# Weight chunks of two of three loaders cast on VectorE, and the third loader issued from ScalarE

## The chip, the cores and the metric

The kernel runs on the 8 cores of one Trainium2 chip (trn2), the same program on each with its own part of the batch, and no exchange between them. The metric is device time in microseconds of the slowest core. Engines: PE is TensorE (matmuls and transposes), ACT is ScalarE, DVE is VectorE, SP is SyncE, which here only issues transfers, POOL is GpSimd, used at the start alone.

## The reference

An input x of 32 sequences of 2048 rows and 1024 columns (f32) goes through four layers, each added to its input:

```python
x = x + attn_a(layernorm(x))   # q, k = xWq+bq, xWk+bk; softmax(q k^T / 32) + eye - mean; times layernorm(x)
x = x + ffn(layernorm(x))      # sigmoid(xr Wr) * (relu(xk Wk)^2 Wv); xr, xk mix a row with the row before
x = x + attn_b(layernorm(x))   # 8 heads of 128, four segments of 512 rows, a memory M, z carried on
x = x + ffn(layernorm(x))      # the same weights as the first ffn
```

Each weight is 1024 x 1024 in f32: wqa and wka of the first attention, wr, wkf and wvf of the FFN, wqb, wkb and wvb of attention b.

## The kernel before

A core computes four sequences, one after the other. A sequence lies whole in SBUF (`x_tm`, 16 tiles of 128 rows, f32), and goes through attention a, FFN (f1), attention b (ab) and FFN (f2) there. Products are in bf16.

**Order.** The program is written out by hand by a planner (`Plan`): each call appends an instruction to the list of its engine, with the semaphore values that it waits for. An engine runs its list strictly in this order, so an instruction that waits holds up all that stands behind it. `dv`, `ac`, `mm_group`, `tr_group` append to DVE, ACT and PE; `sy_dma` and `sc_dma` append a transfer to SP's and to ACT's list. `sy_dma` waits for all earlier transfers of SP (semaphores sXD, sST), and `sc_dma` for all earlier ones of ACT (sGD), so each of the two lists has one transfer in flight.

**Weights.** SBUF has room for three weights in bf16 (`warena`, slots 0 to 2), and they are loaded anew for each layer of each sequence. A `LoadW` loads one in 8 steps, from chunk c = 7 down to 0: a step transfers 128 x 1024 in f32 (512 KB) to a staging place and casts it to bf16 into `warena[:, slot, c, :]`. The staging place is the free front part of the slot itself for c >= 2, and the shared buffer `wst0` for c = 1 and 0, where a transfer waits for the cast that used it before (`buf_war["wst"]`). A step's transfer waits for the cast of the step before. q = 0 has the transfer issued by SP, q = 1 by ACT. The cast was ACT's `activation(Identity)` in both cases (L305). `arm` puts a loader on a list with a gate, all that PE, ACT and DVE have been given up to then; `wstep()` makes one step of each armed loader at this place of the program, and `fin()` the steps that are left.

**Where the steps stand.**

- At the start of the kernel `LKA.fin()` loads wka in 8 steps, ahead of the normalised tiles.
- In the scores loop of attention a, 16 tiles c in four groups of four (order 2, 3, 0, 1): each tile has `wstep()`, `emit_scores` (four products for one bank each, banks 0 and 1 in turn, each freed by an exp on ACT, L537), and `emit_tail` of the tile before (DVE's L549, L553 and L556 make `nzcol`, which PE transposes; PE transposes the exps, DVE copies them (L580), PE multiplies, DVE adds to `x_tm` (L596), then `stats_tile`: DVE's sum L348 and ACT's square L351). Groups 0 and 1 of the loop carry the 8 steps of wkf, group 3 four steps of wr, groups without a loader none.
- After the loop wvf is armed and has one step behind the last tail; `emit_ffn` finishes wr and wvf with `fin()` right after `ln_stats` and before the normalised tiles (`ln_apply`: even tiles on ACT L415, odd ones on DVE L419), for which PE's transposes wait.
- The FFN runs per group of 512 rows: `s12` (normalise, transpose, mix), `s3` (products with wr and wkf), `s4` (8 products with wvf, each evacuated by DVE's L763 out of banks 0 and 1 in turn; then per tile transposes back, two DVE adds L784, and a hook). In the last `s4` there is a `wstep()` ahead of each of the 8 products: wqb and wkb after f1, the next sequence's wqa and wka after f2. The hook after f1 is `stats_tile`; after f2 it stores the tile, loads the next sequence's tile in its place, both on SP, and takes `stats_tile` of that.
- wvb is armed after the last `s4` of f1, and `fin()` in `emit_attn_b` makes all its 8 steps, after `ln_stats` and before two memsets and the normalised tiles.
- Attention b handles a segment head by head: `passA_g(h + 1)` and `passB_g(h)` are interleaved, with a `wstep()` ahead of each h. In the last segment wr, wkf and wvf for f2 are armed together, so each of the 8 steps handles three chunks. `passB_g` begins with two ACT operations (L987, L991) and DVE's L994.

Of the kernel before, what the change touches and what calls it, by code (L numbers as in the profile page):

```python
# [9 lines left out]
AF = mybir.ActivationFunctionType  # L10
# [79 lines left out]
def build_nc(n_sub=4, dbg=False, ffn_level=None):  # L90
# [11 lines left out]
    wvfT_d = nc.dram_tensor("wvfT", [D, D], F32, kind="ExternalInput").ap()  # L102
    wqb_d = nc.dram_tensor("wqb", [D, D], F32, kind="ExternalInput").ap()
    wkb_d = nc.dram_tensor("wkb", [D, D], F32, kind="ExternalInput").ap()
    wvb_d = nc.dram_tensor("wvb", [D, D], F32, kind="ExternalInput").ap()
# [19 lines left out]
    warena = sb("warena", [P, 3, NC, D], BF16)  # L125
# [68 lines left out]
    def dv(fn, waits=(), tag="", inc=True):  # L194
        return p_.add("vector", fn, waits=waits, inc=("sDV" if inc else None), tag=tag)

    def ac(fn, waits=(), tag="", inc=True):
        return p_.add("scalar", fn, waits=waits, inc=("sAC" if inc else None), tag=tag)
# [30 lines left out]
    def gp_dma(out, in_, waits=(), tag=""):  # L229
        waits = list(waits) + [p_.cur("sGD")]  # L230
        def f(e, out=out, in_=in_):
# [10 lines left out]
       waits=[m1], tag="identb")  # L242
# [4 lines left out]
       waits=[mt], tag="tril")  # L247
# [4 lines left out]
       waits=[m2], tag="identf")  # L252
# [13 lines left out]
                              func=AF.Sigmoid), waits=[sm_ready], tag="gate")  # L266
# [6 lines left out]
       tag="negbq")  # L273
    dv(lambda e: e.tensor_scalar(out=dsm[:, 7, :], in0=smalls[:, 5, :],
                                 scalar1=-1.0, scalar2=None, op0=ALU.mult),
       tag="negbk")
# [5 lines left out]
    class LoadW:  # L282
# [7 lines left out]
        def step(self):  # L290
            if self.c < 0:
                return
            c = self.c
            self.c -= 1
            dma = sy_dma if self.q == 0 else sc_dma
            wf = warena.ap()[:, self.slot, :, :].rearrange(
                "p c e -> p (c e)").bitcast(F32)
            stage = wf[:, 0:1024] if c >= 2 else wst0.ap()
            w = list(self.gate) + ([self.last] if self.last else [])
            if c < 2:  # L300
                w = w + buf_war.get("wst", [])
            ld = dma(stage, self.dram_ap[128 * c:128 * (c + 1), :], waits=w,
                     tag=f"{self.tag}c{c}")
            self.last = ac(lambda e, slot=self.slot, c=c, stage=stage:
                           e.activation(out=warena[:, slot, c, :], in_=stage,  # L305
                                        func=AF.Identity),
                           waits=[ld], tag=f"{self.tag}x{c}")
            if c < 2:
                buf_war["wst"] = [self.last]
            if self.c < 0:  # L310
                self.mile = self.last
# [25 lines left out]
    for b in range(BL):  # L337
        if n_sub >= 4 and b > 0:
            x_ready = []
        else:  # L340
            xw = [p_.cur("sST")]
            x_mile = sy_dma(x_tm[:], x_d[b].rearrange("(t p) d -> p t d", p=P),
                            waits=xw, tag=f"ldx{b}")
# [93 lines left out]
        def fm_transpose_group(g, buf, src_tiles, xn_m, tag, guard_from=None):  # L437
            miles = []
            tm = None
            for half in range(4):  # L440
# [17 lines left out]
                else:  # L458
                    def f(e, bnk=bnk, buf=buf, dc0=dc0):
# [9 lines left out]
                              tag=f"b{b}ln1_")  # L469
# [8 lines left out]
        if n_sub >= 2:  # L478
            f1_ldrs = (LoadW(wrT_d, 0, 0, f"b{b}f1_ldwr"),
                       LoadW(wkfT_d, 1, 1, f"b{b}f1_ldwk"),  # L480
                       LoadW(wvfT_d, 2, 0, f"b{b}f1_ldwv"))
        else:
            f1_ldrs = None
        w_ka = LKA.fin()
# [7 lines left out]
        for g in range(NG):  # L492
            fm_m, _ = fm_transpose_group(g, g % 2, [4 * g + t for t in range(4)],
                                         xn_m[4 * g + 2:4 * g + 4],
                                         tag=f"b{b}a1g{g}")
            for ec in range(NC):
# [4 lines left out]
                def f(e, bnk=bnk, ec=ec, g=g):  # L501
# [4 lines left out]
                                    tag=f"b{b}Kev{g}_{ec}"))  # L506
# [4 lines left out]
        for dh in range(2):  # L511
# [3 lines left out]
                          tag=f"b{b}cs{dh}")  # L515
# [92 lines left out]
        for gi, g in enumerate([2, 3, 0, 1]):  # L608
            if gi >= 2:
# [3 lines left out]
                                             tag=f"b{b}a2g{g}")  # L613
# [3 lines left out]
            for ec in range(NC):  # L617
# [4 lines left out]
                def f(e, bnk=bnk, ec=ec):  # L622
# [4 lines left out]
                                 tag=f"b{b}Qev{g}_{ec}"))  # L627
            if gi == 3 and f1_ldrs:
                arm(f1_ldrs[0], slot_free_gate())
            for c4 in range(4):  # L630
                c = 4 * g + c4
# [503 lines left out]
        if n_sub >= 3:  # L1135
            ab_ldrs = (LoadW(wqb_d, 0, 0, f"b{b}ab_ldwq"),
                       LoadW(wkb_d, 1, 1, f"b{b}ab_ldwk"),
                       LoadW(wvb_d, 2, 0, f"b{b}ab_ldwv"))
        f2_ldrs = None
        if n_sub >= 4:  # L1140
            f2_ldrs = (LoadW(wrT_d, 0, 0, f"b{b}f2_ldwr"),
                       LoadW(wkfT_d, 1, 1, f"b{b}f2_ldwk"),
                       LoadW(wvfT_d, 2, 0, f"b{b}f2_ldwv"))
        nseq = None
        if n_sub >= 4 and b + 1 < BL:
            carry_qa = LoadW(wqaT_d, 0, 0, f"b{b + 1}ldwqa")
# [28 lines left out]
        if n_sub < 4:  # L1175
            st_w = p_.barrier_waits("sDV", "sAC", "sPE")
            sy_dma(out_d[b].rearrange("(t p) d -> p t d", p=P), x_tm[:],
                   waits=st_w, store=True, tag=f"st{b}")
# [3 lines left out]
           waits=[("sST", 16 * NSTORE), p_.cur("sGD"), p_.cur("sXD")],  # L1182
           tag="final")
# [66 lines left out]
if __name__ == "__main__":  # L1250
    nc = build_nc()
    print("built OK")
```

How the kernel before makes its waits and increments, by code:

```python
    def hard_barrier(tag=""):  # L210
        arr = {}
        for e in ("tensor", "vector", "scalar", "gpsimd"):
            s = p_.eng_sem[e]
            def mk(s=s):
                return lambda en: en.sem_inc(sems[s], 1)
            arr[e] = p_.add(e, mk(), inc=s, tag=f"{tag}barA", attach=False)
        dmaw = [p_.cur("sGD"), p_.cur("sXD"), p_.cur("sST")]
        allw = list(arr.values()) + dmaw
        for e in ("tensor", "vector", "scalar", "gpsimd", "sync"):
            p_.add(e, (lambda en: en.wait_ge(sems["sGP"], 1)), waits=allw,
                   tag=f"{tag}barW")
# [969 lines left out]
            def body(eng):  # L1191
                for (fn, w, incs, tag) in p_.ops[eng_name]:
                    for (s, v) in w:
                        eng.wait_ge(sems[s], v)
                    inst = fn(eng)
                    for (s, v, a) in incs:
                        if a:
                            inst = inst.then_inc(sems[s], v)
```

## Time and profile before

| | us |
|---|---|
| two timed runs | 9316.83 and 9549.73 |
| their median | 9433.28 |
| the profiled execution | 9315.16 |
| its span on the slowest core (core 2) | 9313.5 |
| spans of cores 0 to 3 | 9287.9 to 9313.5 |
| spans of cores 4 to 7 | 9217.3 to 9237.7 |
| PE busy | 5086.6 (55%) |
| DVE busy | 3046.4 (33%) |
| ACT busy | 2712.0 (29%) |
| mean granted TensorE clock, core 2 and core 6 | 0.725 and 0.735 |

The profile is of one execution. "Busy" leaves out issuing and waiting; idle time of an engine is listed with what ended it, the releaser. Lines such as L305 are lines of the kernel; ACTq and SPq are the issues of transfers by ACT and SP. The granted clock is a share of full speed, 1.0 for 2.4 GHz and 0.5 for 1.2 GHz.

### The profile page before, as it was taken

The numbers are of one execution on the slowest core, as the hardware profiler recorded it, in microseconds if no ns is written. First come the engines' busy times: TensorE is split into PE (matmuls) and PEld (weight loads), VectorE is DVE, ScalarE is ACT, GpSimd is POOL, SyncE is SP. The second block draws the span as 40 slices with busy tenths as digits, with TensorE's granted clock in tenths as the row PEclk, the third lists the DMA queues.
The fourth block names the chain that finished last, engine by engine and source line by source line (L and its number), as shares of the span: only waits on it lengthen the run. The fifth ranks groups of instructions, "written<-read, shape, count | busy, mean of one in ns | idle before, by whom it ended". The sixth has DMA issues, their size and how long they took to land.

```text
span 9313.5 us, 79467 instructions; the slowest of 8 cores (9217.3 to 9313.5 us)
## 1 busy us (share of the span) xinstructions
PE 5086.6 (55%) x26253; PEld 2480.5 (27%) x26688; DVE 3046.4 (33%) x6569; ACT 2712.0 (29%) x4642; POOL 8.6 (0%) x14
## 2 busy tenths in 40 slices
PE   3856444435586644443558563444355866444437
PEld 1323222212232322221223232222122323222213
DVE  2124244343112424434312242443431124244343
ACT  3222333321322233332132223333213222333321
POOL 0000000000000000000000000000000000000000
PEclk9988766667798866666779786555677977755558
DMA  2010100111101010011110101001011010100000
GB/s 73 19 37 1 55 1 1 32 35 43 57 17 37 1 55 1 1 39 34 36 59 14 37 7 48 1 1 39 34 36 57 16 37 1 55 1 1 25 30 37
DMA packets 69421, 256.82 MB, mean 28 GB/s; under 512 B 7584, under 2 KB 7584, under 8 KB 69024
## 3 DMA queue, kind: packets, MB, share of 16 engines
q1 hardware_dynamic: 50592, 184.60, 6.0%
q10 hardware_dynamic: 18432, 67.12, 2.3%
q8 instruction: 225, 3.69, 0.2%
q14 instruction: 172, 1.41, 0.1%
HBM read 218.14 MB, written 33.55 MB: 27 GB/s over the span
## 4 chain that ended last, share of the span: by engine, by line
PE 45%; DVE 18%; ACT 13%; DMA 12%; issue 10%; DVEq 1%; ACTq 0%; SPq 0%
PE pb L170 37%; PE pb L183 6%; DVE a L699 4%; PE pb L943 2%; ACT warena L305 2%; DMA x_tm<-x 2%; DMA warena<-wkfT 2%; DVE a L692 2%; ACT xn_fm L460 1%; ACT xn_tm L991 1%; DMA out<-x_tm 1%; ACT ptbuf L928 1%; ACT xn_tm L987 1%; DVE ebuf L911 1%; DMA warena<-wqb 1%
## 5 line engine op out<-in xcount | busy, mean ns | idle before, releaser
L170 PE MATMUL pb<-a,warena 128*128 128x512 bf16 x6013 | 1431.1, 396 | 372.1 <-DVE a L699 157.6
L170 PE MATMUL pb<-xn_fm,warena 128*128 128x512 bf16 x5000 | 1209.5, 405 | 92.7 <-ACT xn_fm L460 59.2
L170 PEld LDWEIGHTS pb<-a,warena 128*128 128x128 bf16 x6144 | 613.5, 101 | 1167.5 <-issue 580.3
L183 PE MATMUL pb<-identb,xn_tm 128*128 128x128 bf16 x2304 | 243.0, 281 | 1098.9 <-ACT xn_tm L415 780.2
L183 PE MATMUL pb<-identb,ebuf 128*128 128x128 bf16 x2304 | 285.8, 261 | 1009.7 <-DVE ebuf L911 1009.7
L351 ACT ACTIVATE junkb<-x_tm 128x1024 bf16<-128x1024 f32 x256 | 270.4, 1056 | 1935.1 <-DMA x_tm<-x 688.1
L170 PE MATMUL pb<-ebuf,warena 128*128 128x512 bf16 x1992 | 529.5, 430 | 420.6 <-DVE a L763 387.8
L170 PEld LDWEIGHTS pb<-xn_fm,warena 128*128 128x128 bf16 x5120 | 523.3, 103 | 765.8 <-issue 344.6
L183 PEld LDWEIGHTS pb<-identb,xn_tm 128*128 128x128 bf16 x2304 | 200.0, 127 | 1150.3 <-issue 1148.0
L170 PE MATMUL pb<-xn_tm,ptbuf 128*128 128x512 bf16 x1984 | 458.0, 384 | 81.1 <-DVE ptbuf L580 76.1
L905 ACT ACTIVATE ebuf<-pb 128x128 bf16<-128x128 f32 (+3 forms) x512 | 221.5, 433 | 924.2 <-PE pb L170 698.3
L183 PEld LDWEIGHTS pb<-identb,ebuf 128*128 128x128 bf16 x2304 | 165.0, 109 | 1159.2 <-issue 1154.6
L348 DVE TENSOR_REDUCE stats<-x_tm 128x1 f32<-128x1024 f32 x256 | 306.3, 1217 | 439.7 <-DMA x_tm<-x 424.1
L170 PE MATMUL pb<-a 128*128 128x128 bf16 (+4 forms) x2496 | 430.9, 271 | 7.8 <-DVE xn_tm L1006 7.8
L305 ACT ACTIVATE warena<-warena 128x1024 bf16<-128x1024 f32 x264 | 275.7, 1054 | 488.2 <-DMA warena<-wkfT 109.5
L170 PEld LDWEIGHTS pb<-ebuf,warena 128*128 128x128 bf16 x2048 | 219.2, 109 | 725.6 <-issue 566.0
L862 ACT ACTIVATE a<-pb,smalls_s 128x512 bf16<-128x512 f32 x384 | 263.8, 687 | 483.9 <-PE pb L170 483.9
L699 DVE SCALAR_TENSOR_TENSOR a<-xn_fm,smalls_s,a 128x512 bf16<-128x512 bf16 x512 | 384.6, 751 | 54.9 <-DVE a L692 1.8
L943 PE MATMUL pb<-xn_tm,ptbuf 128*128 128x128 bf16 x1280 | 215.9, 291 | 335.6 <-ACT ptbuf L928 183.3
L743 DVE TENSOR_TENSOR ebuf<-ebuf 128x4096 bf16<-128x4096 bf16 x32 | 73.3, 2292 | 914.0 <-ACT ebuf L733 914.0
L183 PE MATMUL pb<-identf,a 128*128 128x128 f32 x1024 | 173.9, 314 | 348.7 <-DVE x_tm L784 318.5
L456 DVE COPY xn_fm<-pb 128x1024 bf16<-128x1024 bf16 x144 | 99.4, 691 | 676.8 <-PE pb L183 676.8
(101 smaller groups left out, 5286.1 us busy)
## 6 DMA issues: line engine op xcount, KB each, us to landing
out<-x_tm SPq DMA_DIRECT2D x64, 512.0 KB, 2.6
warena<-wkfT ACTq DMA_DIRECT2D x48, 512.0 KB, 3.5
warena<-wrT SPq DMA_DIRECT2D x48, 512.0 KB, 3.6
warena<-wvfT SPq DMA_DIRECT2D x48, 512.0 KB, 3.4
x_tm<-x SPq DMA_DIRECT2D x48, 512.0 KB, 3.5
warena<-wqaT SPq DMA_DIRECT2D x24, 512.0 KB, 4.3
warena<-wkaT ACTq DMA_DIRECT2D x24, 512.0 KB, 3.6
warena<-wqb SPq DMA_DIRECT2D x24, 512.0 KB, 4.7
```

The lines of the kernel that those rows point to most:

```text
L170: return e.matmul(out, lhsT, rhs, start=st, stop=sp)
L183: return e.transpose(out, in_, ident)
L305: e.activation(out=warena[:, slot, c, :], in_=stage, func=AF.Identity),
L348: s1m = dv(lambda e, i=i: e.tensor_reduce(stats[:, i, 0:1], x_tm[:, i, :], axis=AX.X, op=ALU.add), waits=w, tag=f"{tag}S1_{i}")
L351: s2m = ac(lambda e, i=i: e.activation(out=junkb.ap(), in_=x_tm[:, i, :], func=AF.Square, accum_out=stats[:, i, 1:2]), waits=w + buf_war.g ...
L456: return e.tensor_copy(xn_fm[:, buf, dc0:dc0 + 2, 4:516], pbb[bnk][:, 0:1024])
L460: return e.copy(xn_fm[:, buf, dc0:dc0 + 2, 4:516], pbb[bnk][:, 0:1024])
L692: e.tensor_scalar(out=xrxk[:, u, dc, :], in0=xn_fm[:, buf, dc, 3:515], scalar1=dsm[:, omcol, dc:dc + 1], scalar2=None, op0=ALU.mult),
L699: e.scalar_tensor_tensor(out=xrxk[:, u, dc, :], in0=xn_fm[:, buf, dc, 4:516], scalar=smalls[:, mucol, dc:dc + 1], in1=xrxk[:, u, dc, :], o ...
L862: e.activation(out=sqkv[:, u, ec, :], in_=pb[bnk].ap(), func=AF.Identity, bias=smalls[:, bcol, ec:ec + 1]),
L905: e.activation(out=Eslot[:, 0:ncols], in_=pb[sb_].ap()[:, 0:ncols], func=AF.Exp, scale=1.0 / np.sqrt(DK)),
L943: return e.matmul(pb[4].ap()[:, 128 * lc:128 * lc + 128], ptbuf[:, j, :], xn_tm[:, 4 + j, 128 * h:128 * h + 128], start=st, stop=sp)
```

## The change

- A loader with q = 1 has its cast made by DVE (`tensor_copy`) instead of ACT; one with q = 0 keeps ACT's `activation`.
- wvf (f1 and f2) and wvb change from q = 0 to q = 1: their transfers are issued by ACT, and their casts are DVE's.

The steps stand where they stood, and the order of all else is the same.

```diff
--- before.py
+++ after.py
@@ -301,10 +301,15 @@
                 w = w + buf_war.get("wst", [])
             ld = dma(stage, self.dram_ap[128 * c:128 * (c + 1), :], waits=w,
                      tag=f"{self.tag}c{c}")
-            self.last = ac(lambda e, slot=self.slot, c=c, stage=stage:
-                           e.activation(out=warena[:, slot, c, :], in_=stage,
-                                        func=AF.Identity),
-                           waits=[ld], tag=f"{self.tag}x{c}")
+            if self.q == 0:
+                self.last = ac(lambda e, slot=self.slot, c=c, stage=stage:
+                               e.activation(out=warena[:, slot, c, :],
+                                            in_=stage, func=AF.Identity),
+                               waits=[ld], tag=f"{self.tag}x{c}")
+            else:
+                self.last = dv(lambda e, slot=self.slot, c=c, stage=stage:
+                               e.tensor_copy(warena[:, slot, c, :], stage),
+                               waits=[ld], tag=f"{self.tag}x{c}")
             if c < 2:
                 buf_war["wst"] = [self.last]
             if self.c < 0:
@@ -478,7 +483,7 @@
         if n_sub >= 2:
             f1_ldrs = (LoadW(wrT_d, 0, 0, f"b{b}f1_ldwr"),
                        LoadW(wkfT_d, 1, 1, f"b{b}f1_ldwk"),
-                       LoadW(wvfT_d, 2, 0, f"b{b}f1_ldwv"))
+                       LoadW(wvfT_d, 2, 1, f"b{b}f1_ldwv"))
         else:
             f1_ldrs = None
         w_ka = LKA.fin()
@@ -1135,12 +1140,12 @@
         if n_sub >= 3:
             ab_ldrs = (LoadW(wqb_d, 0, 0, f"b{b}ab_ldwq"),
                        LoadW(wkb_d, 1, 1, f"b{b}ab_ldwk"),
-                       LoadW(wvb_d, 2, 0, f"b{b}ab_ldwv"))
+                       LoadW(wvb_d, 2, 1, f"b{b}ab_ldwv"))
         f2_ldrs = None
         if n_sub >= 4:
             f2_ldrs = (LoadW(wrT_d, 0, 0, f"b{b}f2_ldwr"),
                        LoadW(wkfT_d, 1, 1, f"b{b}f2_ldwk"),
-                       LoadW(wvfT_d, 2, 0, f"b{b}f2_ldwv"))
+                       LoadW(wvfT_d, 2, 1, f"b{b}f2_ldwv"))
         nseq = None
         if n_sub >= 4 and b + 1 < BL:
             carry_qa = LoadW(wqaT_d, 0, 0, f"b{b + 1}ldwqa")
```

## Rows read from the trace of the kernel before

**Rows 1.** Head of the page and its part 1: busy us (share), instructions

```profile
span 9313.5 us, 79467 instructions; the slowest of 8 cores (9217.3 to 9313.5 us)
...
PE 5086.6 (55%) x26253; PEld 2480.5 (27%) x26688; DVE 3046.4 (33%) x6569; ACT 2712.0 (29%) x4642; POOL 8.6 (0%) x14
```

**Rows 2.** List of waits (engine line <- releaser: us, times, longest); grouped lines

```profile
PE pb L183 <- ACT xn_tm L415: 780.2, 16, 102.0
...
L305 ACT ACTIVATE warena<-warena 128x1024 bf16<-128x1024 f32 x264 | 275.7, 1054 | 488.2 <-DMA warena<-wkfT 109.5
```

**Rows 3.** Grouped lines, DVE's cast from f32 to bf16 in SBUF

```profile
L1129 DVE CAST a<-a 128x1024 bf16<-128x1024 f32 x16 | 11.1, 694 | 1.7
```

**Rows 4.** Timeline (start us, us, what), scores loop of the first sequence

```profile
296.02 0.33 ACTq L226 DMA_DIRECT2D warena<-wkfT  x1
299.58 1.06 ACT L305 ACTIVATE warena<-warena 128x1024 bf16<-128x1024 f32 x1 [2.51 <-DMA warena<-wkfT]
...
317.09 0.67 ACT L623 ACTIVATE warena<-pb,smalls_s 128x512 bf16<-128x512 f32 x1
...
420.00 0.69 ACT L623 ACTIVATE warena<-pb,smalls_s 128x512 bf16<-128x512 f32 x1 [3.80 <-PE pb L170]
...
451.04 1.06 ACT L351 ACTIVATE junkb<-x_tm 128x1024 bf16<-128x1024 f32 x1 [10.27 <-DVE x_tm L596]
...
456.98 0.22 PE L183 MATMUL pb<-identb,nzcol 128*1 128x128 bf16 x1
...
510.11 0.69 ACT L623 ACTIVATE warena<-pb,smalls_s 128x512 bf16<-128x512 f32 x1 [3.81 <-PE pb L170]
```

**Rows 5.** Timeline, last products of the first FFN to attention b

```profile
967.12 1.06 ACT L305 ACTIVATE warena<-warena 128x1024 bf16<-128x1024 f32 x1 [1.10 <-DMA warena<-wqb]
...
973.09 1.06 ACT L305 ACTIVATE warena<-warena 128x1024 bf16<-128x1024 f32 x1 [1.27 <-DMA warena<-wqb]
...
975.13 0.69 DVE L763 TENSOR_TENSOR a<-pb,xn_tm 128x512 f32<-128x512 f32 x1 [1.03 <-PE pb L170]
...
985.65 1.22 DVE L348 TENSOR_REDUCE stats<-x_tm 128x1 f32<-128x1024 f32 x1
...
1011.63 1.06 ACT L305 ACTIVATE warena<-wst 128x1024 bf16<-128x1024 f32 x1 [3.84 <-DMA wst<-wkb]
...
1024.85 1.04 ACT L305 ACTIVATE warena<-warena 128x1024 bf16<-128x1024 f32 x1
...
1058.09 1.06 ACT L305 ACTIVATE warena<-wst 128x1024 bf16<-128x1024 f32 x1 [3.69 <-DMA wst<-wvb]
...
1061.66 3.75 PE L183 MATMUL pb<-identb,xn_tm 128*128 128x128 bf16 x32 [77.40 <-ACT xn_tm L415]
```

**Rows 6.** Timeline, end of the first sequence, start of the second's loads

```profile
2397.03 0.34 SPq L206 DMA_DIRECT2D out<-x_tm  x1
...
2401.85 1.06 ACT L305 ACTIVATE warena<-wst 128x1024 bf16<-128x1024 f32 x1 [3.75 <-DMA wst<-wkaT]
```

**Rows 7.** Timeline, last segment of attention b in the first sequence

```profile
1790.91 0.33 ACTq L226 DMA_DIRECT2D warena<-wkfT  x1
...
1799.01 1.23 DVE L994 SCALAR_TENSOR_TENSOR a<-a,xn_tm 128x1024 bf16<-128x1024 bf16 x1 [5.80 <-ACT xn_tm L991]
...
1910.38 0.33 ACTq L226 DMA_DIRECT2D wst<-wkfT  x1
...
1921.81 1.23 DVE L994 SCALAR_TENSOR_TENSOR a<-a,xn_tm 128x1024 bf16<-128x1024 bf16 x1 [11.10 <-ACT xn_tm L991]
```

**Rows 8.** Timeline, first loads of the kernel

```profile
94.86 0.33 ACTq L226 DMA_DIRECT2D wst<-wkaT  x1
...
98.47 1.06 ACT L305 ACTIVATE warena<-wst 128x1024 bf16<-128x1024 f32 x1 [3.69 <-DMA wst<-wkaT]
```

**Rows 9.** Windows: us, busy us of PE PEld DVE ACT POOL, PEclk, DMA, GB/s

```profile
5902.00:5925.00 23.00, 22.91 (x83) 9.29 (x83) 0.00 (x0) 6.87 (x10) 0.00 (x0) 0.77 0.00 1
...
1280.00:1303.00 23.00, 22.91 (x98) 10.13 (x99) 0.00 (x0) 8.12 (x12) 0.00 (x0) 0.93 0.00 1
```

## The prediction

> **What bounds the kernel now.** I read the page's head first: 9313.5 us of span, PE busy for 55% of it, DVE 33%, ACT 29% [rows 1]. No engine is full, so the time lies in waits, and what an edit is worth has to be read at the places where the load instructions stand. The second view is the list of waits, with the grouped lines: PE waits 780.2 us in 16 places for ACT's L415, the normalised tile at the head of a stage, up to 102 us at once, and ACT's 264 casts of L305 through `warena` stand behind 488.2 us of idle ACT [rows 2]. ACT runs its instructions in order: a load step (`LoadW.step`) on it is an issue, a wait for the landing, and a cast of 1.05 us. The third view is the timeline around the load steps. They stand in five kinds of place: inside the scores loop of the first attention (A), at the start of the first FFN (B), from the last `s4` of an FFN to the next stage (C towards attention b, E towards the next sequence), in the last segment of attention b (D), and once at the start of the kernel (F).
>
> **What the change moves.** wka, wkf and wkb are issued by ACT as before, but cast by DVE. wvf and wvb are now issued by ACT instead of SP, and cast by DVE. wqa, wr and wqb stay as they are. ACT no longer waits for those landings; DVE does, in its own order. ACT's next issue waits for DVE's cast, and also for the landing of its previous transfer (`sc_dma` waits on sGD), so two ACT loads never overlap. SP's queue loses 96 issues of 0.33 us, ACT's gets them; they lie in waits and I cost them at nothing.
>
> **Price of a cast.** DVE has no cast of a weight chunk now. Its nearest row is L1129, f32 to bf16, 128x1024, SBUF to SBUF: 694 ns [rows 3]. I take 0.69. The ends are 0.35 (half of it) and 1.05, what ACT takes [rows 2]. Of the 224 casts that move (wka and wkb 32 each, wkf 64, wvf 64, wvb 32) only those in a serial chain count, some 15 per sequence, so the ends move the sum by about 20 us each way.
>
> **A, the scores loop: 8 wkf steps per sequence.** Four tiles with a step take 102.91 us (317.09 to 420.00), four without one 90.11 us (420.00 to 510.11): 12.8 us for four steps [rows 4]. The other four steps stand in the first group, where two of them come before any tail (`emit_tail`); all hold back the exps that free the two score banks. I take 11.5, between 6.4 (two steps only) and 12.8. The cover on DVE: the issue comes at 296.02 and the cast can start at 299.58, 3.56 later [rows 4]. A DVE cast then ends 4.3 us after the issue, and three small DVE operations (about 0.5) give `nzcol` at 4.9. PE asks for it when its score groups are done, 456.98 against a square at 451.04, thus 5.9 us after [rows 4]. So the stall is hidden by about 1 us, and without cover it would cost the excess 32 times. A = -4 x (12.8 + 11.5) = -97 us.
>
> **B, start of the first FFN.** The first wvf step now makes DVE wait some 3.7 us ahead of the statistics, where SP had fetched it long before. Seven more steps form a chain whose cast is 0.37 shorter, -2.6. DVE's two normalised tiles then follow the chain instead of ACT's two, 0.7 shorter. Sum about +0.5 per sequence, +2 in all; from -1 to +4 each.
>
> **C, last `s4` before attention b.** Now the eight products need DVE only for the evacuation L763, whose last one starts at 975.13, and DVE is through with the tiles at 986.87 (985.65 + 1.22), 11.7 us later [rows 5]. The eight pairs of load steps run on ACT beside this until 1012.7. After the change each `wstep` puts a DVE wait in front of one evacuation. Do the steps get faster? Wq's casts are 5.97 us apart (967.12, 973.09), and before each ACT waits 1.1 to 1.3 us for wq's own transfer, although the cast of wk already stands in between [rows 5]. So wq's transfer sets the pace, and the last wk step stays near 1011.3 (0.3 off for a shorter cast). Then: DVE cast ends 1012.0, the 11.7 us of the tail follow, 1023.7; the statistics take the 7.2 they take now (1017.65, which is 1012.7 plus four squares, to 1024.85) and 1.0 more, since their first DVE steps were done ahead: 1031.9. Then wvb: issue to cast 3.61 [rows 8], and steps of 4.75 now ((1058.09 - 1024.85)/7), less 0.37 = 4.38 [rows 5]. Last cast at 1031.9 + 3.6 + 7 x 4.38 = 1066.2, ended 1066.9, then memsets (1.9) and two tiles (1.6) on DVE, which were hidden: PE starts at 1070.4 instead of 1061.66 [rows 5]. C = +8.8 x 4 = +35 us.
>
> The Trainium skill (DMA: Bandwidth & Descriptors, Issuing engines are not separate DMA queues) says that transfers started by different engines run on the same DMA engines and interleave, so that a second issuer saves sequencer time alone. By that rule wq's pace would stay as it is, and the trace's 5.97 agrees; with a pace of 4.75 the sum would be that of the first rival below.
>
> **E, last `s4` before the next sequence, three times.** The first store of the last four tiles waits in SP's queue behind the last wqa transfer, and goes at 2397.03; the last wka cast starts at 2401.85 [rows 6]. After: that cast is on DVE, ahead of the last evacuation, and ends at 2402.1; evacuation 0.7, transposes 0.9 with the two adds 1.3: the store goes at 2405.1. The four store-and-load pairs are serial behind it. E = +8.1 x 3 = +24 us.
>
> **D, last segment of attention b, 8 steps of three loads.** ACT issues wk at 1790.91, and DVE's next own operation, L994, starts at 1799.01, 8.1 later: wk's landing, three ACT casts and the two exps lie between [rows 7]. After: wk lands 3.9 after its issue, only then ACT issues wv, 3.6 to land, 0.69 to cast: 8.3. The exps are ready before that (ACT goes on 1.6 earlier than now). So a step costs +0.2 to +0.9; I take +0.4. The last two steps share `wst0` and are serial now: 1910.38 to 1921.81 is 11.4 [rows 7], after 3.5 + 0.7 + 3.6 + 0.7 = 8.5, so -2.9 each. D = 4 x (6 x 0.4 - 2 x 2.9) = -14 us. The cover is DVE's idle time ahead of L994; if a landing is late, all of it shows.
>
> **F, start.** ACT is free after the last issue of wka (94.86) instead of after the cast (98.47 + 1.06) [rows 8]: 4.7, and the chain is 7 x 0.37 = 2.6 shorter. F = -7 us.
>
> **Sum.** -97 + 2 + 35 + 24 - 14 - 7 = -57 us. The profiled execution took 9315.16 us, so 9258. The two timed runs are 9316.83 and 9549.73, median 9433.28; the profiled one stands with the lower, and the sum is made against it.
>
> **Rivals.**
> 1. ACT, freed of wk's waits, does speed up the wq chain in C and E, from 5.97 to 4.75 over five intervals, 6 us at 7 places, -42: 9216. For it: in some pairs of E ACT still holds the cast of wq back. Against: the 1.1 to 1.3 us that ACT waits for wq itself. 0.15.
> 2. DVE becomes the late engine in D: wv's landing takes 4.7, as wq's does beside another transfer, instead of 3.6. +1.1 x 24 = +26: 9284. It turns the whole change into a loss from 2.4 us a step on (57 / 24). 0.15.
> 3. A does not come: nzcol is late in the scores loop. The cover is 1 us; each further us costs 32, and half of A lost (landings of 5.9) gives 9306. Against it: this queue's landings beside nothing else are even. 0.05.
> 4. The other side: PE, now with fewer gaps in the scores loop, is granted less clock. Row: 83 matmuls in 23 us at a clock of 0.77, against 98 in 23 us at 0.93 for the same projection of attention b in the first sequence [rows 9], 18% longer. On the two groups of A, about 162 us after the change, it is 29 us a sequence, +117: 9375. It decides from half of that (57 us) on. Against: four tiles without a step already fill PE and still take 90.11 us [rows 4]. 0.07. The Trainium skill (TensorE: Matmul & The Clock Gate, Part 1) tells of a limiter that takes a whole die to 13/16 of the clock once three of its cores run dense matmuls; by that rule the 0.77 is such a stretch, and these cores all run this loop together.
> 5. The moves cancel because C and E cost twice what I have, 59 us more: 9317. 0.08.
>
> **Chances and range.** My forecast has 0.5. Between them the cases run from 9216 to 9375; with the bounds of the cast and of the first group of A, 9200. A median over runs as far apart as the two before can lie up to 117 us above the lower ones, and the upper end takes that in: 9385. 2% of 9315 is 186 us, about what a measurement can tell from no change. Faster by that takes three times my gain, with C and E at nothing and the stalls of D gone too (0.08, partly for the spread of the runs); slower needs rivals 2 and 4 much larger (0.05); within 2% 0.87.
>
> **What would show it.** In the profile after: four tiles of the scores loop with wkf steps take about 90 us, not 103; DVE has 224 casts near 0.69; ahead of attention b the last evacuation L763 starts about 51 us after the first wqb cast, not 14, and PE's stage starts 109 us after it, not 100; the spacing of L994 in the last segment stays at 23.6 for six steps and falls from 29 to 26 for two; the first store of the last four tiles comes 8 us later after its chain. The prediction is wrong if wq's casts come 4.7 apart, if nzcol holds PE in the scores loop, or if L994 comes late by over 1 us a step.

## The result, and the profile after

The changed kernel takes 9267.6 us (median of 44 runs), the kernel before 9356.9 us (median of 42). In some executions of any of these kernels a die, or both, runs at a lower granted clock and takes some per cent longer: both medians hold such executions, and the ratio and every comparison of times below leave them out. The ratio is 0.994, with a 95% interval of 0.991 to 0.996: a gain of 0.4 to 0.9%, within 2%. The lowest times, 9225.4 before and 9183.0 after, are 42 us apart. The forecast, 9258 against the 9315 of the profiled execution, is the same ratio, 0.994.

The profiled execution takes 9209.7 us. Its slowest core is core 1, with 9208.0. The stages are compared on core 6, whose clock was near that of before (0.732, and 0.735): 9217.3 us before, 9158.6 after, 58.7 less. The forecast's sum was 57 less. The other cores of this die (4, 5 and 7) came out 48.2, 55.0 and 47.4 less: core 6 gained most of the four, so that 58.7 lies so near to 57 is partly the choice of the core.

Head, busy line and the group of the new casts from the page of the kernel after (its casts are L306 on ACT and L311 on DVE, and the lines below them moved by 5), and a line of its list of waits:

```profile
span 9208.0 us, 79961 instructions; the slowest of 8 cores (9158.6 to 9208.0 us)
...
PE 5125.4 (56%) x26688; PEld 2477.0 (27%) x26688; DVE 3193.1 (35%) x6793; ACT 2492.2 (27%) x4418; POOL 8.6 (0%) x14
...
L311 DVE CAST warena<-warena 128x1024 bf16<-128x1024 f32 x168 | 116.5, 694 | 793.4 <-DMA warena<-wkfT 276.0
...
PE pb L183 <- DVE xn_tm L424: 771.8, 46, 97.4
```

224 casts, 4418 ACT instructions instead of 4642, went to DVE, at 694 ns as in [rows 3]. The wait of PE for a stage's first tile is as long as in [rows 2] (771.8 after 780.2), and ends on DVE's L424 now. It got hardly shorter: what was gained was gained in the scores loop.

The table adds up each stage over the four sequences, from the starts of its first and last operation on core 6. "Before" and "after" are us, the last two columns differences.

| stage | before | after | measured | forecast |
|---|---|---|---|---|
| F, to the first group of the scores loop | 230.8 | 223.5 | -7.3 | -7 |
| A, two groups of the scores loop with wkf steps | 746.5 | 651.3 | -95.2 | -97 |
| the two groups without them | 766.6 | 765.9 | -0.7 | 0 |
| B, last square of the loop to the FFN's transposes | 224.7 | 217.6 | -7.0 | +2 |
| C, last s4 to attention b's transposes | 416.8 | 453.2 | +36.4 | +35 |
| attention b, first three segments | 2500.6 | 2498.3 | -2.3 | 0 |
| D, last segment | 1052.8 | 1057.6 | +4.7 | -14 |
| E, last s4 to the next sequence | 346.9 | 364.7 | +17.7 | +24 |
| the rest (both FFNs, starts of sequences 1 to 3) | | | -5.0 | 0 |

**A.** Timeline of the kernel after, core 6, one tile of the scores loop with a wkf step (start us, us, what):

```profile
278.93 1.06 ACT L356 ACTIVATE junkb<-x_tm 128x1024 bf16<-128x1024 f32 x1 [10.28 <-DVE x_tm L601]
279.03 0.33 ACTq L226 DMA_DIRECT2D warena<-wkfT  x1
...
282.61 0.69 DVE L311 CAST warena<-warena 128x1024 bf16<-128x1024 f32 x1 [2.50 <-DMA warena<-wkfT]
...
283.55 0.14 DVE L561 TENSOR_SCALAR nzcol<-zbuf 128x1 bf16<-128x1 f32 x1
...
284.86 0.22 PE L183 MATMUL pb<-identb,nzcol 128*1 128x128 bf16 x1
...
295.99 1.06 ACT L356 ACTIVATE junkb<-x_tm 128x1024 bf16<-128x1024 f32 x1 [10.27 <-DVE x_tm L601]
```

The issue comes at 279.03, DVE's cast at 282.61, nzcol is done at 283.69 and PE takes it at 284.86: 1.2 us of cover, the forecast's "about 1". Tile follows tile after 17.06 us (278.93 to 295.99), as in the groups without a step.

What a step had cost can be taken apart. For each kernel, before and then after, a line of core 6's list of waits over all four sequences, and the window of the third sequence's two groups with steps (length, busy us of PE, weight loads, DVE, ACT and POOL, granted clock, share of DMA, GB/s):

```profile
PE pb L170 <- ACT ebuf L537: 85.0, 48, 3.1
4852.50:5041.50 189.00, 157.74 (x775) 68.88 (x774) 33.18 (x68) 49.58 (x105) 0.00 (x0) 0.95 0.07 23
...
PE pb L170 <- ACT ebuf L542: 10.0, 16, 1.8
4819.90:4982.70 162.80, 150.10 (x774) 67.87 (x773) 38.64 (x76) 42.27 (x96) 0.00 (x0) 0.99 0.08 26
```

PE's waits for a late exp fell from 48 to 16. The 32 that are gone, one for each wkf step, were 74 us, 2.3 each. The other 21 us are PE's own: the same matmuls kept it busy for 621.7 us in these groups before and for 600.4 after (windows of the four sequences), at a granted clock of 0.99 instead of 0.95 in the third. The price of 12.8 us for four steps was read off whole stretches, so the forecast held both parts without telling them apart.

**C.** The same view, the first wqb cast to PE's first transposes of attention b (L768 is the evacuation, L424 the normalised tile, L353 the sum of a tile):

```profile
926.00 1.06 ACT L306 ACTIVATE warena<-warena 128x1024 bf16<-128x1024 f32 x1 [3.64 <-DMA warena<-wqb]
...
973.20 0.69 DVE L311 CAST warena<-wst 128x1024 bf16<-128x1024 f32 x1 [7.69 <-DMA wst<-wkb]
973.81 0.68 DVE L768 TENSOR_TENSOR a<-pb,xn_tm 128x512 f32<-128x512 f32 x1
...
985.03 1.22 DVE L353 TENSOR_REDUCE stats<-x_tm 128x1 f32<-128x1024 f32 x1
...
997.83 0.69 DVE L311 CAST warena<-warena 128x1024 bf16<-128x1024 f32 x1 [2.84 <-DMA warena<-wvb]
...
1028.74 0.69 DVE L311 CAST warena<-wst 128x1024 bf16<-128x1024 f32 x1 [3.69 <-DMA wst<-wvb]
...
1033.22 2.97 PE L183 MATMUL pb<-identb,xn_tm 128*128 128x128 bf16 x24 [49.31 <-DVE xn_tm L424]
```

DVE sat idle for 7.69 us behind the landing of wkb, and the last evacuation, ready long before, came 47.8 us after the first wqb cast (973.81), 11.2 us ahead of the last tile's sum. Before, it came 14.7 us after that cast on core 6, and 14.0 on core 2 (975.13 in [rows 5]); the forecast had 51 for it now. The wvb chain takes 30.91 for seven steps (997.83 to 1028.74), 4.42 each, where it was 4.75.

**E and D.** Timeline, core 6, end of the last s4 of the first f2, and one step of the last segment of attention b:

```profile
2372.48 0.69 DVE L311 CAST warena<-wst 128x1024 bf16<-128x1024 f32 x1 [7.96 <-DMA wst<-wkaT]
2373.09 0.68 DVE L768 TENSOR_TENSOR a<-pb,xn_tm 128x512 f32<-128x512 f32 x1
...
2376.82 0.34 SPq L206 DMA_DIRECT2D out<-x_tm  x1
```

```profile
1810.53 0.33 ACTq L226 DMA_DIRECT2D warena<-wkfT  x1
...
1811.08 1.06 ACT L306 ACTIVATE warena<-warena 128x1024 bf16<-128x1024 f32 x1
...
1812.27 0.33 SPq L206 DMA_DIRECT2D warena<-wrT  x1
1814.02 0.33 ACTq L226 DMA_DIRECT2D warena<-wvfT  x1
1814.04 0.69 DVE L311 CAST warena<-warena 128x1024 bf16<-128x1024 f32 x1 [1.54 <-DMA warena<-wkfT]
1814.45 1.06 ACT L992 ACTIVATE xn_tm<-a 128x1024 f32<-128x1024 bf16 x1 [2.31 <-DMA warena<-wkfT]
1815.60 1.06 ACT L996 ACTIVATE xn_tm<-xn_tm 128x1024 f32<-128x1024 f32 x1
...
1818.78 0.69 DVE L311 CAST warena<-warena 128x1024 bf16<-128x1024 f32 x1 [4.04 <-DMA warena<-wvfT]
1819.39 1.22 DVE L999 SCALAR_TENSOR_TENSOR a<-a,xn_tm 128x1024 bf16<-128x1024 bf16 x1
...
1843.52 1.22 DVE L999 SCALAR_TENSOR_TENSOR a<-a,xn_tm 128x1024 bf16<-128x1024 bf16 x1
```

In E the first store goes 4.3 us after the last wka cast; in [rows 6] it went 4.8 ahead of it. In D the two transfers of ACT stand one after the other (1810.53, and 1814.02 when wk has landed), wv's cast comes 4.76 us after its issue, and L999 starts 8.86 us after wk's issue, where L994 came 8.1 after it in [rows 7]. By then the second exp (L996) has been done for 2.7 us: the wait is for wv alone. The next L999 is 24.13 us later, against 23.2 before.

### The profile page after: what moved, and what is told of

Read it like the earlier page. It is cut to its first block, busy times and chain, and to the rows that moved or that the text cites. A ratio compares the mean times of both kernels' runs of the same rounds, so it can differ in the third digit from the quotient of the medians.

```text
span 9208.0 us, 79961 instructions; the slowest of 8 cores (9158.6 to 9208.0 us)
## 1 busy us (share of the span) xinstructions
PE 5125.4 (56%) x26688; PEld 2477.0 (27%) x26688; DVE 3193.1 (35%) x6793; ACT 2492.2 (27%) x4418; POOL 8.6 (0%) x14
## 4 chain that ended last, share of the span: by engine, by line
PE 47%; DVE 20%; DMA 13%; ACT 10%; issue 9%; DVEq 1%; ACTq 0%; SPq 0%
PE pb L170 38%; PE pb L183 6%; DVE a L704 4%; PE pb L948 2%; DMA x_tm<-x 2%; DMA warena<-wvfT 2%; DVE a L697 2%; DMA out<-x_tm 1%; ACT xn_fm L465 1%; ACT ptbuf L933 1%; DVE ebuf L916 1%; DVE x_tm L789 1%; DVE xn_tm L1055 1%; ACT xn_tm L996 1%; DMA warena<-wqb 1%
## 5 line engine op out<-in xcount | busy, mean ns | idle before, releaser
L170 PE MATMUL pb<-xn_fm,warena 128*128 128x512 bf16 x5120 | 1168.1, 392 | 79.0 <-ACT xn_fm L465 51.5
L170 PE MATMUL pb<-ebuf,warena 128*128 128x512 bf16 x2048 | 568.5, 443 | 529.9 <-DVE a L768 503.0
L183 PE MATMUL pb<-identb,xn_tm 128*128 128x128 bf16 x2304 | 237.9, 276 | 982.1 <-DVE xn_tm L424 771.8
L170 PE MATMUL pb<-a 128*128 128x128 bf16 (+4 forms) x2560 | 468.2, 278 | 7.8 <-DVE xn_tm L1011 7.8
L353 DVE TENSOR_REDUCE stats<-x_tm 128x1 f32<-128x1024 f32 x256 | 306.4, 1217 | 359.7 <-DMA x_tm<-x 344.2
L748 DVE TENSOR_TENSOR ebuf<-ebuf 128x4096 bf16<-128x4096 bf16 x32 | 73.4, 2292 | 921.5 <-ACT ebuf L738 921.5
L311 DVE CAST warena<-warena 128x1024 bf16<-128x1024 f32 x168 | 116.5, 694 | 793.4 <-DMA warena<-wkfT 276.0
L1065 PE MATMUL pb<-xn_tm 128*128 128x128 bf16 x512 | 135.5, 265 | 325.4 <-DVE xn_tm L1055 325.4
```

The source lines that it names most:

```text
L170: return e.matmul(out, lhsT, rhs, start=st, stop=sp)
L183: return e.transpose(out, in_, ident)
L311: e.tensor_copy(warena[:, slot, c, :], stage),
L353: s1m = dv(lambda e, i=i: e.tensor_reduce(stats[:, i, 0:1], x_tm[:, i, :], axis=AX.X, op=ALU.add), waits=w, tag=f"{tag}S1_{i}")
L1065: return e.matmul(pb[mb].ap()[:, 128 * (h % 4):128 * (h % 4) + 128], xn_tm[:, 8 + lc, 128 * h:128 * h + 128], vdp, start=st, stop=(h % 4 = ...
```

## The experiments

My theory: the gain is wkf's casts off ACT in the scores loop; C and E lose because a landing now stands ahead of an evacuation on DVE; D neither gains nor loses because the issue order (ACT, one transfer in flight) took what the casts gave. Rivals: an effect of the two parts of the change together, an accident of the clock, and the rivals of the forecast. All experiments start from the changed kernel; `LoadW` got a parameter that names the engine of the cast ("ac" or "dv") apart from q. Stage differences to before, in us over four sequences, on core 6 (for "wvf of f2 on SP" core 2 of that kernel, against core 6 before):

| kernel | A | B | C | D | E |
|---|---|---|---|---|---|
| after | -95.2 | -7.0 | +36.4 | +4.7 | +17.7 |
| A alone | -94.7 | -1.8 | -3.6 | +3.5 | -4.4 |
| C and E undone | -92.4 | -5.6 | +3.8 | +5.3 | -1.7 |
| wvf of f2 on SP | -78.8 | -3.8 | +38.3 | -94.0 | +19.4 |
| issue only | +3.0 | +3.7 | +15.0 | +90.8 | +0.3 |
| cast only | -94.0 | -18.1 | +27.7 | -90.4 | +19.3 |
| casts of A four times | -42.2 | -1.5 | +45.1 | +8.3 | +24.3 |
| C with wkb alone | -93.8 | -6.3 | +28.0 | +6.5 | +17.5 |
| each part where it pays | -92.9 | -16.3 | +2.1 | -111.1 | -2.1 |

Stages that no edit touches differ by up to 6 us between these executions, and once by 9 (C, with the casts of A repeated): differences of that size are not read.

**A alone.** Every loader but wkf of f1 is as before.

```diff
-            LKA = LoadW(wkaT_d, 1, 1, f"b{b}ldwka")
+            LKA = LoadW(wkaT_d, 1, 1, f"b{b}ldwka", "ac")
-                       LoadW(wvfT_d, 2, 1, f"b{b}f1_ldwv"))
+                       LoadW(wvfT_d, 2, 0, f"b{b}f1_ldwv", "ac"))
...
```

The loaders wkb, wvb, wkf and wvf of f2, and the next wka are set back in the same way.

> The kernel before, with the casts of the first FFN's wkf (the loader stepped in the scores loop) alone moved to DVE; everything else as before. Theory (place A is the gain, and it is ACT's wait in front of the exps): the two groups with steps lose 95 us in all, as in the changed kernel, nothing else moves, ratio 0.990. Rival (a fuller PE is granted less clock and gives it back): the groups lose less, or later stages grow, and the ratio is 0.995 or more.

A is -94.7 us, alone as together, and no other stage of the table moved by more than 5. Spans are 9115.8 to 9144.8. So the 32 wkf casts of the scores loops are worth more than the whole change, and the other edits together cost some 40 us.

**C and E undone.** wkb, wvb and the next sequence's wka as before, the rest changed.

```diff
-                       LoadW(wkb_d, 1, 1, f"b{b}ab_ldwk"),
-                       LoadW(wvb_d, 2, 1, f"b{b}ab_ldwv"))
+                       LoadW(wkb_d, 1, 1, f"b{b}ab_ldwk", "ac"),
+                       LoadW(wvb_d, 2, 0, f"b{b}ab_ldwv", "ac"))
-            carry_ka = LoadW(wkaT_d, 1, 1, f"b{b + 1}ldwka")
+            carry_ka = LoadW(wkaT_d, 1, 1, f"b{b + 1}ldwka", "ac")
```

> The changed kernel, with wqb's partner wkb, wvb and the next sequence's wka handled as before (casts on ACT, wvb issued by SP). Theory (DVE's waits ahead of the last s4's evacuations cost 36 us at C and 18 at E): it is 54 us faster than the changed kernel and 112 faster than before, ratio to before 0.988. Rival (C and E cost nothing, since ACT's chain was the bound there anyway): it equals the changed kernel, ratio 0.994.

The times that can be compared are 9139.6 to 9162.1, the ratio to before is 0.987 (0.978 to 0.997; 0.988 expected). C and E are back at their times of before (+3.8, -1.7): their +54 are these three loaders' alone.

**wvf of f2 on SP.** Its cast stays on DVE, its issue goes back to SP.

```diff
-                       LoadW(wvfT_d, 2, 1, f"b{b}f2_ldwv"))
+                       LoadW(wvfT_d, 2, 0, f"b{b}f2_ldwv", "dv"))
```

> The changed kernel, with the second FFN's wvf issued by SP again, but cast by DVE. Theory (in the last segment of attention b the wait is that of one ACT transfer for the one before it, on one queue): SP has wvf landed before the step, L999 comes 4 us earlier per step in six of eight steps, 24 us a sequence, 96 in all; ratio to before 0.983. Rival (the two exps on ACT or PE end last there): the steps stay within 1 us of the changed kernel's 24.4.

D falls from +4.7 to -94.0: one edit of a queue is worth 99 us. The mean granted clock of that core was 0.711, against 0.735 before, so its -78.8 in A is not read, nor is a ratio. D can be: "cast only", at 0.735, has -90.4 there with the same handling of wvf, and with each core set against itself before, all eight lie between -79 and -110.

**Issue only.** All casts back on ACT, all issues as changed.

```diff
-                       LoadW(wkfT_d, 1, 1, f"b{b}f1_ldwk"),
-                       LoadW(wvfT_d, 2, 1, f"b{b}f1_ldwv"))
+                       LoadW(wkfT_d, 1, 1, f"b{b}f1_ldwk", "ac"),
+                       LoadW(wvfT_d, 2, 1, f"b{b}f1_ldwv", "ac"))
...
```

The other loaders with q = 1 get "ac" in the same way.

> One part of the change alone: wvf and wvb issued by ACT, all casts on ACT. Theory: A, C and E stay as before; in the last segment of attention b the transfers of wkf and wvf are serial with both casts on ACT, +3.8 us a step over six steps (23.3 to 27), +91 us in all, and the start of the first FFN +4 a sequence: +106, ratio 1.011. Rival (where the transfer is issued does not matter, only who casts): ratio 1.000.

**Cast only.** The casts as changed, wvf and wvb issued by SP as before.

```diff
-                       LoadW(wvfT_d, 2, 1, f"b{b}f1_ldwv"))
+                       LoadW(wvfT_d, 2, 0, f"b{b}f1_ldwv", "dv"))
...
```

Likewise wvb and wvf of f2.

> The other part of the change alone: wkf, wkb, wka cast by DVE, and wvf, wvb cast by DVE but issued by SP as before. Theory: A as in the changed kernel (-95), the last segment of attention b at -94 instead of +5, E +18, C about +22 (wvb's first landing is hidden again behind the statistics): ratio 0.983. Rival (the moved issue frees SP and is part of the gain): ratio above 0.99.

One step of the last segment, core 6, first with the issues alone changed, then with the casts alone (L993, L997 and L1000 are the two exps and DVE's operation; in both, ACT issued wkf first, at 1804.79 and 1800.49):

```profile
1808.37 0.33 ACTq L226 DMA_DIRECT2D warena<-wvfT  x1
1812.60 1.06 ACT L307 ACTIVATE warena<-warena 128x1024 bf16<-128x1024 f32 x1 [3.19 <-DMA warena<-wvfT]
...
1814.69 1.06 ACT L997 ACTIVATE xn_tm<-xn_tm 128x1024 f32<-128x1024 f32 x1
...
1815.86 1.23 DVE L1000 SCALAR_TENSOR_TENSOR a<-a,xn_tm 128x1024 bf16<-128x1024 bf16 x1 [8.77 <-ACT xn_tm L997]
```

```profile
1800.49 0.34 ACTq L226 DMA_DIRECT2D warena<-wkfT  x1
...
1803.37 1.06 ACT L997 ACTIVATE xn_tm<-xn_tm 128x1024 f32<-128x1024 f32 x1
1803.99 1.30 DVE L312 CAST warena<-warena 128x1024 bf16<-128x1024 f32 x2 [1.25 <-DMA warena<-wkfT]
...
1805.20 1.22 DVE L1000 SCALAR_TENSOR_TENSOR a<-a,xn_tm 128x1024 bf16<-128x1024 bf16 x1
```

Issued by ACT and cast by ACT, both exps stand behind two landings, and L1000 comes 11.1 us after wk's issue: D +90.8. With SP's issue wv has been there since the step before, DVE makes both casts without a second wait, and L1000 comes 4.7 after the issue: D -90.4. The change joined a loss and a gain of the same size, and the forecast saw only their sum. The spans with the casts alone are 9044 to 9067, its lowest time is 9065.2 against 9242.3 for before on the same chip, 0.981 where 0.983 was expected. A and E hang on the cast alone too (A +3.0 with the issues alone). Two expectations failed by more than the scatter: B with the issues alone was to be +16 and is +3.7, and the -18.1 of B with the casts alone was not expected at all. C with the casts alone is +27.7, where 22 was expected. Not foreseen was C with the issues alone, +15.0: wvb's first cast comes 16.8 us after the last wkb cast, where it was 13.2 to 13.6. SP had sent wvb ahead of the statistics; ACT can send it only behind them, and its landing (3.6) lies open four times.

**Casts of A four times.** Each wkf cast of f1 is made four times over (`self.rep` is 4 for that loader and 1 for the others).

```diff
-                self.last = dv(lambda e, slot=self.slot, c=c, stage=stage:
-                               e.tensor_copy(warena[:, slot, c, :], stage),
-                               waits=[ld], tag=f"{self.tag}x{c}")
+                for _r in range(self.rep):
+                    self.last = dv(lambda e, slot=self.slot, c=c, stage=stage:
+                                   e.tensor_copy(warena[:, slot, c, :], stage),
+                                   waits=[ld] + ([self.last] if _r else []), tag=f"{self.tag}x{c}")
```

> The changed kernel, with each cast of the first FFN's wkf made four times in a row on DVE (the same result), 2.2 us more of DVE ahead of nzcol in the scores loop. Theory (cover of about 0.9 us ahead of nzcol): 1.3 us show in five tiles of eight per sequence, the two groups with steps grow by 26 us in all against the changed kernel. Rival (DVE has no cover there): all 2.2 us show in five tiles or more, 45 us or more. Rival (cover far larger): nothing shows.

A is 53 us longer than after: by the number the first rival's (45 or more), not the 26 of the theory. Timeline of a step on core 6, a line of the list of waits over all four sequences, then the window of the third sequence's two groups with steps, two tiles of them, and a tile of the kernel after:

```profile
282.99 0.33 ACTq L226 DMA_DIRECT2D warena<-wkfT  x1
...
286.74 3.08 DVE L314 CAST warena<-warena 128x1024 bf16<-128x1024 f32 x4 [2.67 <-DMA warena<-wkfT]
...
290.35 0.22 PE L183 MATMUL pb<-identb,nzcol 128*1 128x128 bf16 x1 [1.46 <-DVE nzcol L564]
```

```profile
PE pb L183 <- DVE nzcol L564: 42.9, 28, 2.7
```

```profile
4869.40:5047.70 178.30, 157.19 (x774) 69.48 (x773) 55.31 (x100) 42.29 (x97) 0.00 (x0) 0.95 0.08 24
4909.70:4930.20 20.50, 17.74 (x84) 7.62 (x83) 7.31 (x14) 3.76 (x11) 0.00 (x0) 0.92 0.08 26
4930.20:4948.80 18.60, 16.05 (x85) 7.19 (x84) 7.29 (x14) 3.80 (x11) 0.00 (x0) 1.00 0.11 29
```

```profile
4941.01:4958.07 17.06, 15.96 (x84) 7.18 (x83) 5.15 (x10) 3.78 (x11) 0.00 (x0) 1.00 0.10 32
```

The mechanism is the theory's all the same. Four of the 28 waits for nzcol stand behind the loop and were there before the change as well (10.8 us); the 24 of the steps, six a sequence where the theory had five, are 32 us, 1.3 each, where 2.4 us of casts were added. So a cover of about 1.1 us is real, and no wider. At a clock of 1.00 the tile is 1.5 longer (18.60 against 17.06), which is the gap; in others the clock fell too, to 0.92 over the tile, with 20.50. The remaining 21 of the 53 us are that second part: PE is busy for 621.5 us in these groups, with the same matmuls, instead of 600.4, and the granted clock over the third sequence's is back at the 0.95 of before the change. The theory left it out, the first rival (no cover) is refuted by the 1.3.

**C with wkb alone.** As after, but wvb issued by SP and cast by ACT.

```diff
-                       LoadW(wvb_d, 2, 1, f"b{b}ab_ldwv"))
+                       LoadW(wvb_d, 2, 0, f"b{b}ab_ldwv", "ac"))
```

> The changed kernel with wvb alone handled as before (issued by SP, cast by ACT); wkb stays on DVE. Theory: of the 36 us at C, about 28 (7 a sequence) come from DVE's wkb waits ahead of the evacuations, which push the tail of the last s4 behind the chain, and 8 from wvb's first landing and the two memsets that are no longer hidden; so C is +28 against before. Rival (wvb's move is the cost): C is near 0.

C is +28.0 instead of +36.4. So wkb's casts on DVE cost 28, 7 a sequence, through the evacuation that they hold, and wvb's move 8 (8 to 12 on cores 4, 5 and 7). Its two halves nearly cancel: the open landing and the memsets behind the chain against seven steps at 4.42.

**Each part where it pays.** A as changed; the casts of wvf on DVE with SP's issue in f1 and f2; wkf of f2 issued by SP as well, so that DVE finds both chunks landed; wkb, wvb and the next wka as before.

```diff
-                       LoadW(wvfT_d, 2, 1, f"b{b}f1_ldwv"))
+                       LoadW(wvfT_d, 2, 0, f"b{b}f1_ldwv", "dv"))
-                       LoadW(wkfT_d, 1, 1, f"b{b}f2_ldwk"),
-                       LoadW(wvfT_d, 2, 1, f"b{b}f2_ldwv"))
+                       LoadW(wkfT_d, 1, 0, f"b{b}f2_ldwk", "dv"),
+                       LoadW(wvfT_d, 2, 0, f"b{b}f2_ldwv", "dv"))
...
```

To these come the three edits of "C and E undone".

> A version meant to beat both: casts of wkf (both FFNs) and wvf on DVE, but the second FFN's wkf and wvf and the first one's wvf issued by SP; wkb, wvb and the next sequence's wka as before (ACT). Theory: scores loop -95, the last segment of attention b -124 (a step there costs little more than ACT's one cast, 19.7 us instead of 23.3), C and E at 0, start and first FFN -15: -230 us, ratio 0.975. Rival (SP's one transfer in flight cannot fetch three chunks within a step of 19 us): the last segment stays at -94, ratio 0.979.

```profile
1790.91 1.07 ACT L993 ACTIVATE xn_tm<-a 128x1024 f32<-128x1024 bf16 x1
1791.17 0.33 SPq L206 DMA_DIRECT2D warena<-wrT  x1
1791.36 1.29 DVE L312 CAST warena<-warena 128x1024 bf16<-128x1024 f32 x2
1792.08 1.06 ACT L997 ACTIVATE xn_tm<-xn_tm 128x1024 f32<-128x1024 f32 x1
...
1793.24 1.23 DVE L1000 SCALAR_TENSOR_TENSOR a<-a,xn_tm 128x1024 bf16<-128x1024 bf16 x1 [0.59 <-ACT xn_tm L997]
...
1812.83 1.23 DVE L1000 SCALAR_TENSOR_TENSOR a<-a,xn_tm 128x1024 bf16<-128x1024 bf16 x1 [0.59 <-ACT xn_tm L997]
```

The sum is -221.8 on core 6, where -230 was expected. D is -111.1, between the two values expected: no landing holds DVE in this step, L1000 waits 0.59 for ACT's exp, behind ACT's cast of wr, and comes every 19.6 us. Spans are 8984.7 to 9011.6; its lowest time is 9003.7, against 9242.3 for before (0.974).

The same kernel on another chip:

> The kernel of e7_best, on another chip, for an interval. If the gain is the sum of the stages (A -95, B -16, D -111, C, E and F near nothing), the span of an undisturbed core is near 8995 us as in e7_best, and the ratio to the kernel before is 0.974 to 0.976. If it hung on that one profiled execution, the stages come out differently here: D nearer to -94 (casts of wr or the exps late), and the ratio above 0.98.

The two times that can be compared are 9015.5 and 9025.0, those of before with no core below a mean clock of 0.73 are 9227.1, 9233.2 and 9235.6: 0.977, a little above what was expected. D is -109.8, so the stages do not hang on one execution; A is -81.2, because its first group ran at a granted clock of 0.84 on this core, where the second sequence's ran at 1.00, and took 12 us more. Two times are too few for an interval. Against the lowest time of the changed kernel, 9183.0, the best times of this kernel on the two chips (9003.7 to 9025.0) are 1.7 to 2.0% lower.

## Why the prediction was right, and which of its terms were not

- **A, -97 forecast, -95.2 measured: right, mechanism and size.** Two values were chosen there, the first group's 11.5 us a sequence (measured 11.6, which is 46.3 / 4) and the cover of about 1 us (1.2 in the timeline, 1.1 by "Casts of A four times"). The prediction put the whole price on the held exps; they were 74 of it, and 21 was slower matmuls at a lower clock. Rival 3 (nzcol late) fell; "Casts of A four times" shows it at the place it was put, once the cover is used up. Rival 4, less clock for a fuller PE, came out the other way on core 6: where the gaps went the clock rose, from 0.95 to 0.99, and the two groups without steps kept their time. On cores 2 and 3 the loop of the first sequence ran at a mean clock of 0.86 and took 390.8 and 389.5 us, where core 6 took 354.2 at 0.97; their other sequences took 352.9 to 354.3. Before the change cores 0 and 1 had such loops as well (core 0 at 0.91 with 397.7 and 390.4, after that 375.6 at 0.97), so these 36 us, a third of the rival's 117, are not shown to be the change's.
- **C, +35 forecast, +36.4: right.** The wq chain, which was to keep its pace, did so within 2 us; wkb 7 a sequence and wvb 2, by "C with wkb alone".
- **F, -7 forecast, -7.3.**
- **D, -14 forecast, +4.7: the size of one term was wrong.** The step "wv 3.6 to land" took its landing from a row of a queue that runs alone. Here it landed in 4.7 (4.76 to the cast; 4.2 to 5.0 in the 24 steps of this kind), while SP's transfer of wr, issued at 1812.27, was under way when wv's was issued at 1814.02. That is rival 2's figure, at fewer steps: six of eight, 24.1 to 24.9 us apart instead of 23.2, about 1.1 more where 0.4 was forecast. Two readings beside it were off as well: the 8.1 from wk's issue to DVE's operation was one step's (7.9 in the mean of core 2, 7.8 of core 6; 8.8 after), and wk landed in 3.5, not 3.9. The two steps through `wst0`, where wv landed with nothing beside it in 3.4 to 3.7, gave 2.5 to 3.2, where 2.9 was forecast. The larger miss is one of reading: the forecast never split the step into cast and issue, and so did not see that -90 and +91 lay in it.
- **E, +24 forecast, +17.7: the delay of the evacuation was right, the chain was shorter.** The last wka cast comes 51.3 us after the group's last L748 (mean of three on core 6), where it was 54.0. Rival 1 had said that ACT, freed of wk's waits, would speed up wq's chain by 6 us at seven places. Over all kernels here such a chain (16 casts) takes 53.3 us with wk cast by ACT (84 chains of cores 2 and 6, spread 1.3) and 52.2 with DVE (70 chains, spread 1.4): rival 1 is there, at some 1.2 us instead of 6. The spread of a single chain is larger, so for E alone the 2.7 are not shown to be the change's.
- **B, +2 forecast, -7.0: the price of the first wait was too high.** Timeline, core 6, the first and a later wvf step:

```profile
583.96 0.69 DVE L311 CAST warena<-warena 128x1024 bf16<-128x1024 f32 x1 [3.27 <-DMA warena<-wvfT]
...
622.38 0.69 DVE L311 CAST warena<-warena 128x1024 bf16<-128x1024 f32 x1 [3.75 <-DMA warena<-wvfT]
```

  DVE waits 3.27 ahead of the statistics, but ACT's casts had held the same statistics before, so the wr chain behind them starts 2.5 later, not 3.7. The chains then give back 1.9 and the tail 1.3, in this sequence, whose B is 0.7 shorter. With the issue left to SP nothing is waited for, and B is -18.1 ("cast only"). The -7.0, and the 2 us of C, are near the scatter (cores 4, 5 and 7 have -1.5 to -3.1 in B); the -18.1 is not.
- **Rival 5** (C and E at twice their price) fell: 54 against 59 forecast.

The Trainium skill (DMA: Bandwidth & Descriptors, Issuing engines are not separate DMA queues) says that transfers of different issuers interleave on the same DMA engines. The row in D agrees: the transfer that ran beside another issuer's landed in 4.7 us instead of 3.5.

The sum of -57 met -58.7 with D and B wrong by +19 and -9, E by -6 and unedited stages by -8. The sum was right partly by that: luck, like the choice of core 6. The base of 9315 was an execution whose cores 0 to 3 had a mean clock of 0.725 to 0.726, so 9258 is no time of the changed kernel undisturbed; what was right is the difference.

## What to carry to other kernels

A cast, the wait for its landing and the next issue are three things, and each belongs on the engine where its place in the order costs nothing: price them one by one, above all when a change moves two together. Here the casts gave 90 us in one stage and the moved issue took 91. Ask of each wait put ahead of an instruction what that instruction frees: for PE's operand there was about 1 us of cover, and for the last evacuation none. And count the clock with a gap: of the 95 us that the scores loop gained, 21 were the same matmuls running faster. And let a transfer be issued by the queue that has nothing else to wait for, early enough to have landed before its cast's turn.

## What the runs showed of the hardware

- A transfer of 512 KB landed 3.5 us after its issue in the median where it ran alone, and 4.7 us beside one issued 1.75 us earlier by another engine (4.2 to 5.0 in 24 such steps).
- Short waits of PE in a dense loop went with a lower granted clock: with 32 waits of 2.3 us, or 24 of 1.3, the same matmuls kept PE busy for 621 us, and without them for 600. A tile with such a gap had a clock of 1.00 or of 0.92, and the 0.92 cost more (1.9 us) than the gap (1.5).
- The same chain of 16 loads, with nothing changed in it, took from 50.5 to 57.7 us with casts on ACT and the order unchanged: stage differences below some 5 us need more than one execution.
